# Delta-rule outputs: contiguous transposed writes on VectorE, and 16 stores of 128-byte runs in place of 4 of 1 KB

## The reference, cut to what matters

```
def step(St, inp):                        # 512 tokens, 4 batches, 32 value heads
    q_t, k_t, v_t, g_t, b_t = inp         # 16 key heads, each shared by 2 value heads
    St = St * exp(g_t)
    v_old = einsum('bhk,bhkv->bhv', k_t, St)
    delta = (v_t - v_old) * b_t
    St = St + k_t[..., None] * delta[:, :, None, :]
    o = einsum('bhk,bhkv->bhv', q_t, St)
core = core * rsqrt(mean(core * core) + eps) * norm_weight * silu(z)
x1 = x + core.reshape(B, S, 4096) @ w_out
```

## Time and profile before

| | |
|---|---|
| median of the timed runs | 3355.97 us |
| the profiled execution's own time | 3361.55 us |
| its span | 3359.8 us, 58642 instructions |
| TensorE busy | 3261.2 us (97%) |
| VectorE busy | 2452.5 us (73%) |
| GpSimd / ScalarE busy | 1864.0 us (55%) / 1541.5 us (46%) |
| DMA queue of SyncE | 130704 packets, 220.92 MB, 23.8% of 16 engines' span |
| stores of core_rows | 256 transfers of 128 KB, 2.2 us from issue to landing |
| middle part, about | 65 to 2531 us of the span |

### The profile page before, as it was taken

The page is one execution under the profiler, slowest core; times in us unless marked ns, Lnnn a source line. Parts: engine busy times, 40 slices in busy tenths (PEclk is TensorE's granted clock), DMA queues, the critical chain, the costliest instruction groups (busy, mean ns, idle before and its releaser), DMA issues. The chain is left out here.

```text
span 3359.8 us, 58642 instructions
## 1 busy us (share of the span) xinstructions
PE 3261.2 (97%) x20832; PEld 2280.0 (68%) x20832; DVE 2452.5 (73%) x3622; ACT 1541.5 (46%) x4983; POOL 1864.0 (55%) x1824
## 2 busy tenths in 40 slices
PE   5899999999999999999999999999989999999999
PEld 2577777777777777777777777777766777764444
DVE  6799999999999999999999999999940111024553
ACT  2456555655565556555655565556532000011232
POOL 2677677777777777677767777777740000011132
PEclk8999999999999999999999999999989999999999
DMA  3123222322223222322232222222215222211001
GB/s 100 42 61 76 76 64 58 73 73 64 63 72 77 62 64 65 79 61 63 71 79 66 57 70 74 66 61 69 87 51 210 75 100 91 84 38 63 0 13 38
DMA packets 132287, 231.75 MB, mean 69 GB/s; under 512 B 15872, under 2 KB 81536, under 8 KB 126464
## 3 DMA queue, kind: packets, MB, share of 16 engines
q1 hardware_dynamic: 130704, 220.92, 23.8%
q10 hardware_dynamic: 1296, 7.08, 0.5%
HBM read 156.39 MB, written 71.57 MB: 68 GB/s over the span
## 5 line engine op out<-in xcount | busy, mean ns | idle before, releaser
L718 PE MATMUL acc<-xT,wc 128*128 128x512 f32 x2048 | 937.9, 601 | 2.8 <-PEq L110 2.0
L718 PEld LDWEIGHTS acc<-xT,wc 128*128 128x128 f32 x2048 | 370.9, 191 | 374.7 <-issue 374.1
L1003 DVE SCALAR_TENSOR_TENSOR d_conv<-acc,wc,d_conv 128x511 f32<-128x511 f32 (+2 forms) x768 | 566.5, 738 | 43.2 <-ACT d_conv L1172 34.0
L731 PE MATMUL acc<-wc,xT 128*128 128x256 f32 x2048 | 473.4, 384 | 0.0
L731 PEld LDWEIGHTS acc<-wc,xT 128*128 128x128 f32 x2048 | 379.1, 190 | 46.2
L620 POOL TENSOR_TENSOR d_bf<-d_kks,d_gam 128x512 f32<-128x512 f32 x128 | 160.2, 1273 | 344.3 <-ACT d_kks L1218 344.3
L1522 PE MATMUL acc<-t_area 128*128 128x512 f32 x768 | 334.6, 595 | 1.0 <-ACT t_area L1971 1.0
L1031 DVE STREAM_TRANSPOSE d_em<-d_dm 128x1024 f16<-128x1024 f16 x256 | 314.5, 1228 | 2.2
L2028 POOL TENSOR_SCALAR t_veps<-t_mv 128x1 f32<-128x1 f32 x32 | 9.7, 303 | 544.4 <-DVE t_mv L1767 544.4
L1522 PEld LDWEIGHTS acc<-t_area 128*128 128x128 f32 x768 | 239.3, 314 | 86.6 <-issue 1.6
L1038 DVE TENSOR_TENSOR d_zm<-d_tz,cons 128x512 f16<-128x512 f32 x384 | 258.9, 674 | 52.4 <-PE d_tz L786 47.5
(11 more groups left out here) (227 smaller groups left out, 7171.5 us busy)
## 6 DMA issues: line engine op xcount, KB each, us to landing
d_decay<-decay_rows SPq DMA_DIRECT2D x64, 512.0 KB, 5.6
v_rows<-d_vb SPq DMA_DIRECT2D x256, 128.0 KB, 2.3
d_vn<-v_rows SPq DMA_DIRECT2D x64, 512.0 KB, 3.6
core_rows<-d_ob SPq DMA_DIRECT2D x256, 128.0 KB, 2.2
t_area<-core_rows SPq DMA_DIRECT2D x30, 1024.0 KB, 4.8
wc<-in_w SPq DMA_DIRECT2D x96, 256.0 KB, 2.9
t_x<-in_x SPq DMA_DIRECT2D x4, 1024.0 KB, 9.5
t_area<-in_wout ACTq DMA_DIRECT2D x2, 2048.0 KB, 13.2
```

Of the source, the lines that this page charges most:

```text
L718: last = nc.tensor.matmul(bank(TILE[j])[:, :], wtile(j, k), xT[:, k, r % B * S:(r % B + 1) * S], start=k == 0, stop=k == KT - 1)
L731: last = nc.tensor.matmul(bank(f"z{j}")[:, i * GV * P:(i + 1) * GV * P].rearrange("p (h n) -> p h n", h=GV), xT[:, k, r % B * S + (2 * j + ...
L1003: nc.vector.scalar_tensor_tensor(c[:, d:S], bank(TILE[j])[:, 0:S - d], tap(j, KS - 1 - d), c[:, d:S], ALU.mult, ALU.add).then_inc(taps, 1)
```

## The change

The buffer `ob` and the DRAM tensor `core_rows` get another order of indices: head and chunk outside, the 32 or 128 tokens inside. `flip_o` writes 1024 contiguous floats for each partition. A store must now write runs of 32 floats (128 bytes), 8 of them for each of 32 partitions, and one transfer is made for each quarter q and each block a: 16 transfers of 32 KB in place of 4 of 128 KB. The counts on `stored` grow to 256 for each iteration. The readers in the tail take 128 contiguous floats as weights.

Three further edits come with it. On GpSimd, `p_full` waits in addition for `o_done` and `decayed_keys` for `s_done` of the iteration two before. In the tail, the loads of x and of ctx share one semaphore each, and SyncE waits for each load's end before it issues the next of its kind.

```diff
+STORES = 16 * NC * NC
...
-        vb, ob = sb("vb", [P, NC, GV * NC, 32]), sb("ob", [P, NC, 32, GV * NC])
+        vb, ob = sb("vb", [P, NC, GV * NC, 32]), sb("ob", [P, NC, GV * NC, 32])
...
-                rows = core_dram[b, :, g, :, :].rearrange("(a i) q n -> q i a n", i=32)
+                rows = core_dram[b, :, g, :, :].rearrange("(a i) c (q j) -> q a i c j", i=32, j=32)
                 for q in range(NC):
-                    sp.dma_start(rows[q], ob[q * 32:(q + 1) * 32].rearrange("p a j c -> p a (j c)")).then_inc(stored, 16)
+                    for a in range(NC):
+                        sp.dma_start(rows[q, a], ob[q * 32:(q + 1) * 32, a]).then_inc(stored, 16)
...
-            sp.wait_ge(stored, 64 * ITERS)
+            sp.wait_ge(stored, STORES * ITERS)
...
             def p_full(m, h):
+                wait(pool, o_done, at(back(m, 2), NC, NC))
...
             def decayed_keys(m, h):
+                wait(pool, s_done, at(back(m, 2), 3, 3))
...
-                wait(dve, stored, at(back(s, 1), 64, 64))
-                nc.vector.transpose(ob[:, :, :, :].rearrange("p a j c -> p a c j"), oo[:, :, :, :].rearrange("p h c (a j) -> p a (h c) j", a=NC)).then_inc(o_flipped, 1)
+                wait(dve, stored, at(back(s, 1), STORES, STORES))
+                nc.vector.transpose(ob[:, :, :, :], oo[:, :, :, :].rearrange("p h c (a j) -> p a (h c) j", a=NC)).then_inc(o_flipped, 1)
...
-    core = xT[:, head // GV, 0:2 * S].rearrange("p (n c) -> p n c", c=GV * NC)[:, :, head % GV * NC + t]
+    core = xT[:, head // GV, (head % GV * NC + t) * P:(head % GV * NC + t + 1) * P]
...
             def load_x(b):
-                sp.dma_start(x1[:, b * NC:(b + 1) * NC, :], a["x"][b * NC:(b + 1) * NC].rearrange("t p n -> p t n")).then_inc(x_loaded[b], 16)
+                if b:
+                    sp.wait_ge(x_loaded, 16 * b)
+                sp.dma_start(x1[:, b * NC:(b + 1) * NC, :], a["x"][b * NC:(b + 1) * NC].rearrange("t p n -> p t n")).then_inc(x_loaded, 16)
...
-    args["core"] = nc.dram_tensor("core_rows", (B, P, G, NC, GV * S // NC), F32, kind="Internal").ap()
+    args["core"] = nc.dram_tensor("core_rows", (B, P, G, GV * NC, P), F32, kind="Internal").ap()
```

More of the change, by code:

```diff
@@ L526, in early_load @@
                 if left == 2:
-                    sp.wait_ge(stored, 64 * (B * KT))
-                    sp.dma_start(xT[:, :, 0:2 * S], core_dram[0, :, 0:KT, :, :].rearrange("p g q n -> p g (q n)")).then_inc(early_loaded, 16)
+                    sp.wait_ge(stored, STORES * (B * KT))
+                    sp.dma_start(xT[:, :, 0:2 * S], core_dram[0, :, 0:KT, :, :].rearrange("p g c n -> p g (c n)")).then_inc(early_loaded, 16)
                 if left == 1:
@@ L1418, in tail @@
         ph = [pc[0], pc[1], acc[0], acc[1]]
-        w_weighed, w_loaded, core_loaded, x_loaded, c_loaded = sem("w_weighed"), sems("w_loaded", 4), sems("core_loaded", 3), sems("x_loaded", B), sems("c_loaded", XH)
+        w_weighed, w_loaded, core_loaded, x_loaded, c_loaded = sem("w_weighed"), sems("w_loaded", 4), sems("core_loaded", 3), sem("x_loaded"), sem("c_loaded")
         wh_loaded, xc_loaded, y_loaded, fc_loaded, pj_loaded = (sem(n) for n in ("wh_loaded", "xc_loaded", "y_loaded", "fc_loaded", "pj_loaded"))
@@ L1451, in load_core @@
                 src = a["core"][grp, :, 2 * q:2 * q + 2, :, :]
-                sp.dma_start(core[u % 3], src.rearrange("p g q n -> p (g q n)")).then_inc(core_loaded[u % 3], 16)
+                sp.dma_start(core[u % 3], src.rearrange("p g c n -> p (g c n)")).then_inc(core_loaded[u % 3], 16)
             def load_x(b):
-                sp.dma_start(x1[:, b * NC:(b + 1) * NC, :], a["x"][b * NC:(b + 1) * NC].rearrange("t p n -> p t n")).then_inc(x_loaded[b], 16)
+                if b:
+                    sp.wait_ge(x_loaded, 16 * b)
+                sp.dma_start(x1[:, b * NC:(b + 1) * NC, :], a["x"][b * NC:(b + 1) * NC].rearrange("t p n -> p t n")).then_inc(x_loaded, 16)
             def load_ctx(h):
-                sp.dma_start(cT[h], a["ctx"][:, h, :]).then_inc(c_loaded[h], 16)
+                if h:
+                    sp.wait_ge(c_loaded, 16 * h)
+                sp.dma_start(cT[h], a["ctx"][:, h, :]).then_inc(c_loaded, 16)
             load_core(0)
@@ L1525, in core_of @@
             def core_of(grp, t, q, h):
-                rows = core[(grp * CHUNKS + q - 2) % 3].rearrange("p (g n c) -> p g n c", g=2, c=GV * NC)
-                return rows[:, h // GV, :, h % GV * NC + t]
+                rows = core[(grp * CHUNKS + q - 2) % 3].rearrange("p (g c n) -> p g c n", g=2, c=GV * NC)
+                return rows[:, h // GV, h % GV * NC + t, :]
             def core_ready(u):
@@ L1556, in values @@
             def values(h):
-                pe.wait_ge(c_loaded[h], 16)
+                pe.wait_ge(c_loaded, 16 * h + 16)
                 for b in range(B):
@@ L1754, in add_core @@
                 if t % NC == 0:
-                    dve.wait_ge(x_loaded[t // NC], 16)
+                    dve.wait_ge(x_loaded, t // NC * 16 + 16)
                 dve.wait_ge(summed, t + 1)
```

## The result

| | before | changed |
|---|---|---|
| median of the timed runs | 3356.0 us (3355.91 to 3357.96, 4 runs) | 3335.47 us (3335.05 to 3336.70, 4 runs) |
| ratio, 95% interval | | 0.9937 (0.9925 to 0.9949) |
| the profiled execution's own time | 3361.55 us | 3335.47 us |

The changed kernel is 20.5 us faster; 3338 was predicted. Lines of `delta_rule` move by 1 (SyncE's loads), 2 (`store_o`) or 4 in the changed kernel (`flip_o` L1023 to L1027, `residual` L1062 to L1066, `solve` L860 to L864), and L1522 becomes L1530.

What follows compares the result with a forecast made beforehand. TensorE, 99% busy in the steady part, was taken as the bound; -20.3 + 4.4 - 2.0 = -17.9 us on 3361.55 gives 3343.6, and 5.6 less for the median 3338 us. Range 3332 to 3380, the forecast's own 3332 to 3347.

Steps and rivals of the forecast that it cites:

- The stall of `solve`: In each steady slot TensorE's `solve` waits 0.32 us for the residual behind `flip_o`; removing it gives 61 x 0.32 = 19.5 us.
- What is late next: After the gain the residual is 0.51 us ahead in each slot, so TensorE's own work is late next.
- The drain: At the end of the middle part a flip counts in full; one more has a `solve` behind it: 0.8 us gained.
- The barrier: After the last flip, sixteen store issues take 5.2 us more and the flip gives back 0.8: +4.4 us, uncovered.
- The taps: Convolution taps queued behind the steady stores lose nothing: 128-byte writes at 14 ns stay hidden below 7.0 us of issues.
- Rival (1): Small writes are dear: at 63 ns each, taps come 7.1 us late 15 times; +98, 3454 us; chance 0.28.
- The weights: In the tail, contiguous weight loads save 0.12 us at 16 places behind short transposes: -2 us.
- the new waits: GpSimd's added waits are for events long done and hidden by its idling ahead of the gate: nothing.
- The execution's own time: The profiled execution took 3361.55 us; the median of the runs lies 5.6 us below it, so 3343.6 becomes 3338.
- (2): The transpose `flip_o` is priced by its reading side or size and stays at 2.06 us: +3, 3359 us; chance 0.07.
- (3): Another wait, of the gate or matrix levels, replaces the stall and half is kept: -8, 3348 us; chance 0.13.

Runs made afterwards that it cites:

- the long pad: The changed kernel with one more VectorE instruction, a product of 128x512 constants, between `flip_o` and `residual`: 3355.89 us, ratio 0.9996.

## Why the prediction was right

The parts, measured one by one, add up to the change: the flip -24.6 in the 60 slots, -0.8 at the barrier; sixteen issues +4.9 at the barrier; weights -2.1; short runs +0.5 at the barrier and up to +1.4 in the slots. That is -22.1 to -20.7 us, where the two measurements of the change gave -20.5 and -22.7. The forecast of -17.9 us fell short of both, mainly by the stall, which was taken 5 us too small.

- **The stall of `solve`.** Right in place and cause: it was fixed to each slot, went with the flip, and came back when only the flip was undone. The term was too small: the forecast was 61 x 0.32 = 19.5 us, and the slots lost 37.22 - 36.81 = 0.41 each, 60 x 0.41 = 24.6. I compared every start of TensorE within one slot before and after. Two distances differ: from `khat_turn` to `solve`, which has the 0.31 that I read, and from the first matmul of `solve` to the second, 213 ns before and 112 now. The method looked at the start alone; the 0.10 behind it was missed. The waits view's 0.49, which I had kept as an upper end, was nearer than I gave it credit for.
- **What is late next.** TensorE's own work, as said; in the slots without new weights no wait for another engine is left. The spare was put at 0.83 - 0.32 = 0.51 us and is 0.36. The rows show part of the reason: from the start of the flip to that of the residual it was 1010.75 - 1008.84 = 1.91 us and is 999.59 - 998.42 = 1.17, so the residual starts 0.74 us earlier and not 0.83.
- **The drain.** -0.8 forecast, -2.1 measured; 1.3 us of this I can't assign. The stage scatters: 94.70 and 92.73 us in the two executions of the changed kernel, and 94.8 to 96.8 in the five kernels with the stepped flip, so single executions can't tell 0.8 from 2.1.
- **The barrier.** +4.4 forecast, +4.6 measured. Two errors cancel here, which is luck. The sixteen issues take 7.70 us and not 7.0, so 6.0 more and not 5.2. And the last store's landing did not stay as it was: it came 1.78 us after the end of its issue, with 128 KB, and comes 1.22 after it now, with 32 KB. The flip's 0.8 was returned as expected: 6.0 - 0.6 - 0.8 = 4.6.
- **The taps.** Not later, as forecast, but in one slot of 15, by 0.6 us (72.2 against 71.1 us in all). The reasons held only in part: the write costs 11.6 ns and not 14, but the issues took up to 9.1 us and not 7.0. The taps stayed covered, with some 1.3 us to spare and not 2.0. Rival (1) was wrong in its price: where the stores were doubled, the chain that it describes (stores, taps, ScalarE, `attend`) was followed link by link, and each late us of it cost more than one, 9.3 for 7.0.
- **The weights** -2.0 forecast, -2.1 measured; **the new waits** nothing, as forecast.
- **The execution's own time.** Subtracting the 5.6 us by which the profiled execution lay above its median was right: up to 5 us of it lay ahead of the first flip, where other executions took as little as 181.3 us. Without that the forecast would have been 3343.6.

Rivals (2) and (3) are out: the flip takes 1.25 us, and with the flip alone the whole stall is gone.

## What to carry to other kernels

A wait that recurs once in each slot on the bounding engine is worth about its own length and not the length of what was removed ahead of it; compare the instruction's distance to its predecessor with a like pair that waits for nothing, and look one matmul further too. Before a transfer is cut into more pieces, ask where the issues have cover: here 768 more of them cost at most half a us in 60 slots and 5 us at the one barrier, where half of the last batch could be given to an idle queue. And find what is queued behind the stores with a reader soon after (here 8 KB of taps): giving it its own buffer was worth 9 us more.

## What the hardware showed unexpectedly

- A stall of TensorE for an operand used as weights costs more than the wait. With the wait, the second matmul of `solve` starts 213 ns after the first, without it 112: 0.10 us on top of 0.31. With the long pad, whose wait is shorter (0.21), the 0.10 is the same (214 ns). That the load of the second weights is no longer ahead is my reading; it was not tested apart.
- A 7.4 us stand of TensorE was followed by a granted clock of 0.50, which was back at 1.00 within 5.1 us, and by 2.3 us of further loss in that time. The stands at the barrier, 3.9 to 10.2 us, are followed by slow matmuls as well (16 in 8.56 to 10.04 us, where at 0.429 us each 7.0 would do), but there the core products wait for weights anyhow: the stage behind the restart stayed at 11.0 us.
- A write of 128 bytes took 11.6 ns of a DMA engine, one of 1 KB 63 ns: an eighth of the bytes for less than a fifth of the time.
- Issues back to back on SyncE take 0.42 to 0.45 us in the median, but single ones up to 2.1 us: 34 of 1024 were over 1 us in the changed kernel, 35 with sixteen stores of 1 KB runs, none of 256 before. In the changed kernel's trace each of the 34 begins within 0.5 us of a packet of 16 KB on the queue that brings instructions (q8), and only 22 of the other 990 do. That it is the cause was not tested.
